# Second attention of a two-layer block: keys made for four heads at a time as even and odd halves, five work banks, the maximum pass spread over half slots

## What is computed

```python
q = (q_in @ Wq + bq).reshape(b, sq, 16, 64).transpose(0, 2, 1, 3)
k = (k_in @ Wk + bk).reshape(b, sk, 16, 64).transpose(0, 2, 1, 3)
v = (v_in @ Wv + bv).reshape(b, sk, 16, 64).transpose(0, 2, 1, 3)
q, k = _rope(q), _rope(k)       # turns dims 2i and 2i+1 by an angle of the position
scores = jnp.einsum('bhqd,bhkd->bhqk', q, k) * (1.0 / np.sqrt(64))
scores = jnp.where(valid[:, None, None, :], scores, -jnp.inf)
attn = jax.nn.softmax(scores, axis=-1)
out = jnp.einsum('bhqk,bhkd->bhqd', attn, v)
return out.transpose(0, 2, 1, 3).reshape(b, sq, 1024) @ Wo + bo
```

## Time and profile before

| | |
|---|---|
| runs, median (lowest to highest) | 2943.0 us (2940.43 to 2944.17) |
| profiled execution, its own time | 2939.36 us |
| its span, first to last instruction | 2937.2 us |
| mean granted clock of TensorE | 0.957 |
| share of the span busy: PE, DVE, ACT, POOL | 90%, 68%, 49%, 47% |

### The profile page before, as it was taken

One profiled execution on the slowest core, in us unless ns is written; L12 is line 12 of the kernel. 1 busy time (PEld: TensorE's weight loads), 2 busy tenths in 40 slices (PEclk: granted clock), 3 DMA queues, 4 the chain that ended last, 5 costly groups with the idle time before them and its releaser, 6 DMA issues. The chain is left out here.

```text
span 2937.2 us, 82056 instructions
## 1 busy us (share of the span) xinstructions
PE 2638.0 (90%) x32600; PEld 1569.0 (53%) x32600; DVE 2006.5 (68%) x6348; ACT 1450.8 (49%) x2243; POOL 1374.3 (47%) x1221
## 2 busy tenths in 40 slices
PE   3679999999989569999999999999999999996598
PEld 2423333333355536666666666666666666664365
DVE  3468888888856567667766766766667667662655
ACT  2247777777744035546446455455464454443222
POOL 2000000000000038877878878878778788785100
PEclk8789999999989779999999999999999999998799
DMA  5421111111010110000000000000000000001000
GB/s 156 144 89 24 24 27 22 25 22 25 21 30 1 64 37 7 19 13 7 18 13 7 17 13 7 26 5 19 13 8 18 13 7 7 7 2 51 0 0 15
DMA packets 109630, 75.20 MB, mean 26 GB/s; under 512 B 43907, under 2 KB 101579, under 8 KB 108752
## 3 DMA queue, kind: packets, MB, share of 16 engines
q1 hardware_dynamic: 109264, 70.08, 8.5%
HBM read 56.61 MB, written 13.43 MB: 24 GB/s over the span
## 5 line engine op out<-in xcount | busy, mean ns | idle before, releaser
L1485 ACT ACTIVATE a_probs<-psS 128x1024 f32<-128x1024 f32 (+1 forms) x448 | 431.7, 964 | 630.0 <-PE psS L1366 625.9
L645 ACT ACTIVATE a_probs<-psS 128x1024 f32<-128x1024 f32 (+2 forms) x512 | 443.5, 866 | 207.0 <-PE psS L586 206.6
L1802 POOL TENSOR_TENSOR a_acc<-a_acc,a_probs 128x512 f32<-128x512 f32 x320 | 407.3, 1273 | 225.1 <-ACT a_probs L1485 221.9
L1389 PE MATMUL psX<-a_probs,a_values 128*64 128x256 f32 x3328 | 445.6, 385 | 1.6
L672 DVE CUSTOM_DVE_ANT_0 a_junk<-psT,a_mask 128x384 f16<-128x384 f32 (+1 forms) x683 | 378.2, 573 | 61.3 <-PE psT L562 41.6
L1804 POOL TENSOR_TENSOR a_acc<-a_acc,a_probs 128x512 f32<-128x512 f32 x320 | 407.1, 1272 | 25.1
L1646 DVE CUSTOM_DVE_ANT_0 a_junk<-psT,a_mask 128x400 f16<-128x400 f32 (+1 forms) x514 | 282.6, 573 | 153.8 <-PE psS L1341 86.3
L1646 DVE CUSTOM_DVE_ANT_0 a_junk<-psS,a_mask 128x400 f16<-128x400 f32 (+1 forms) x510 | 280.7, 573 | 150.9 <-PE psT L1341 88.3
L974 POOL MEMSET r_ones<- 128x128 f16 x1 | 0.2, 205 | 694.4 <-POOLq L719 694.4
L1389 PEld LDWEIGHTS psX<-a_probs,a_values 128*64 128x64 f32 x3328 | 224.1, 137 | 105.2 <-issue 24.6
L1776 POOL TENSOR_TENSOR a_klo<-a_kt,a_khi 128x400 f16<-128x400 f32 (+1 forms) x256 | 242.7, 948 | 18.6 <-ACT a_khi L1537 18.6
(11 more groups left out here) (332 smaller groups left out, 5561.4 us busy)
## 6 DMA issues: line engine op xcount, KB each, us to landing
a_kd<-p_kst SPq DMA_DIRECT2D x24, 416.0 KB, 3.4
a_wq<-in_wq SPq DMA_DIRECT2D x64, 128.0 KB, 2.1
a_keys<-a_kd SPq DMA_DIRECT2D x96, 75.0 KB
p_ctx<-in_ctx SPq DMA_DIRECT2D x8, 768.0 KB
a_ctx<-in_ctx SPq DMA_DIRECT2D x8, 768.0 KB
a_queries<-a_lowest SPq DMA_DIRECT2D x256, 0.5 KB, 2.0
p_mask_raw<-in_mask_t SPq DMA_DIRECT2D x16, 224.0 KB, 4.4
a_queries<-a_qd SPq DMA_DIRECT2D x64, 52.0 KB
```

The source lines that it names most:

```text
L645: nc.scalar.activation(dst, src, ACT.Exp).then_inc(exp_done, 1)
L1389: ins = nc.tensor.matmul(w.sums[n % 2][64 * hd:64 * hd + 64, 0:T], w.values[:, n % 2, c, 64 * hd:64 * hd + 64], w.probs[:, k % RING1, 2 * ...
L1485: nc.scalar.activation(dst, src, ACT.Exp).then_inc(exp_done, 1)
L1802: nc.gpsimd.tensor_tensor(acc, acc, src[:, :, 0, :], ALU.add).then_inc(sum_step, 1)
```

## The change

1. **Quads.** Keys and queries are made for four heads (a quad, two pairs, `QUADS1` = 32) at a time. The columns of `Wk` and `Wq` are put in the order: all even dimensions of four heads, then all odd ones, so one bank holds 4 x 32 even dimensions and the other the odd ones. The exchanged matrix `wk1x` goes. The rotation works between the two banks: four products and two sums per quarter. In even iterations quarters 0 and 1 of a quad are made, in odd ones quarters 2 and 3, at (slot, half) (0, 0) and (3, 1); the queries in even iterations at (6, 1).
2. **Moved by DMA.** ScalarE and GpSimd put the high part and the remainder into `made_keys` and `made_queries`; SP moves each head's even and odd 32 rows from there to its place in `keys` and `queries`, in four transfers for each group of quarters (32 partitions, high and low parts of up to 801 keys each). TensorE, and ScalarE before it overwrites `made_keys`, wait for these transfers (`keys_in`).
3. **Five banks.** The separate banks of the weighed sums become one (`psO`); the bank so freed joins the ring (`NEAR1` = 5). `spread` becomes a piece of the ring. ScalarE copies the weighed sums away (`take_out`) before the next pair's first weighing; `take_inverse` goes.
4. **Half slots.** TensorE's and VectorE's loops run over (slot, half). Scores stand in half 0, weighing in half 1. The eight units of the maximum pass stand alone at (1,1), (2,0), (2,1), (3,0), (4,1), (5,0), (5,1), (6,0); the values in four blocks. `turn_max` stands at (2, 1). ScalarE's loop still runs over slots.

The diff, cut to its core:

```diff
-AHEAD1 = [2, 2, 1, 1, 1, 1, 0]
-VALUES1 = {2: (0, 1), 4: (2, 3)}
-ITERATIONS1 = range(-3, PAIRS1 + 1)
+HALVES1 = [(sl, half) for sl in range(SLOTS1) for half in range(2)]
+UNITS1 = {(1, 1): 0, (2, 0): 1, (2, 1): 2, (3, 0): 3, (4, 1): 4, (5, 0): 5, (5, 1): 6, (6, 0): 7}
+VALUES1 = {(1, 0): 0, (3, 0): 1, (4, 0): 2, (6, 1): 3}
+KEY_TIMES1 = {(0, 0): 0, (3, 1): 1}
+NEAR1 = 5
+ITERATIONS1 = range(-4, PAIRS1 + 1)
...
+            def give_keys(n, js):
+                sp.wait_ge(k_lo, 4 * (n // 2) + js[-1] + 1)
+                made, at0 = made_at(js[0])
+                o, width = QUARTER_AT[js[0]], sum(QUARTER[j] for j in js)
+                for src, dst, part in blocks(n):
+                    sp.dma_start(w.keys[dst, n % KEPT1, :, o:o + width],
+                                 made[src, :, part, at0:at0 + width]).then_inc(keys_in[n % KEPT1][part_of(n, js[0])], 16)
...
+                    if sl == 0 and is_pair(it + 3):
+                        if it >= 1:
+                            sp.wait_ge(b_full, SLOTS1 * it)
+                        give_queries(it + 3)
+                        give_keys(it + 3, (0, 1))
+                        if it % 2 == 0:
+                            give_keys(it + 3, (2, 3))
+                    if it % 2 == 1 and sl in (2, 5) and is_pair(it + 3):
+                        give_keys(it + 3, (2 if sl == 2 else 3,))
...
+                c0 = (2 * (q % 4) + part) * P
                 for i, (split, moving) in enumerate(((0, hi), (1, hi), (0, lo))):
-                    for hd in range(2):
-                        c0 = p * P + 64 * hd
-                        ins = nc.tensor.matmul(out[64 * hd:64 * hd + 64, 0:width], w.wk[:, part, split, c0:c0 + 64], moving,
-                                               start=(i == 0), stop=(i == 2), skip_group_check=True)
+                    ins = nc.tensor.matmul(out[:, 0:width], w.wk[:, split, c0:c0 + P], moving, start=(i == 0), stop=(i == 2))
...
             for it in ITERATIONS1:
-                for sl in range(SLOTS1):
-                    if is_pair(it):
+                for sl, half in HALVES1:
+                    if half == 0 and is_pair(it):
                         scores(it, sl)
...
+                    if half == 1 and sl > 0 and is_pair(it):
+                        weigh(it, sl - 1)
+                    if is_pair(it + 2) and (sl, half) in UNITS1:
+                        for hd in range(2):
+                            ahead(it + 2, UNITS1[sl, half], hd)
...
-                    if is_pair(it + 1) and sl == 1:
+                    if is_pair(it + 1) and (sl, half) == (2, 1):
                         turn_max(it + 1)
...
+            def key_hi(q, j):
+                for part in range(2):
+                    act.wait_ge(near_free[bank_of(("key", q, j, part))], uses_of(("key", q, j, part)))
+                if q > 0:
+                    wait_given(act, 2 * q - 2, j)
+                    wait_given(act, 2 * q - 1, j)
...
                     if is_pair(it):
                         exponent(it, sl)
+                    if is_pair(it - 1) and sl == 0:
+                        take_out(it - 1)
...
                     if is_pair(it + 1) and sl == 1:
                         take_max(it + 1)
-                    if is_pair(it - 1) and sl == 4:
-                        take_inverse(it - 1)
...
+                nc.vector.scalar_tensor_tensor(w.swung[:, 0, 0:width], even, bias[:, 0:1], w.sin[:, cols], ALU.add, ALU.mult)
+                nc.vector.scalar_tensor_tensor(even, even, bias[:, 0:1], w.cos[:, cols], ALU.add, ALU.mult)
+                nc.vector.scalar_tensor_tensor(w.swung[:, 1, 0:width], odd, bias[:, 1:2], w.sin[:, cols],
+                                               ALU.add, ALU.mult).then_inc(k_step, 1)
+                dve.wait_ge(k_step, 2 * done + 1)
+                nc.vector.tensor_tensor(w.kt[:, j % 2, 0, 0:width], even, w.swung[:, 1, 0:width],
+                                        ALU.subtract).then_inc(near_free[bank_of(names[0])], 1)
+                nc.vector.scalar_tensor_tensor(odd, odd, bias[:, 1:2], w.cos[:, cols], ALU.add, ALU.mult).then_inc(k_step, 1)
+                dve.wait_ge(k_step, 2 * done + 2)
+                nc.vector.tensor_tensor(w.kt[:, j % 2, 1, 0:width], odd, w.swung[:, 0, 0:width],
+                                        ALU.add).then_inc(near_free[bank_of(names[1])], 1)
```

More of the change, by code:

```diff
@@ L1097, in leaves_in, with quad_in, quarter_in, split_in @@
     return it // PER_BATCH - 1 if it % PER_BATCH == 0 and it >= PER_BATCH else None
+def quad_in(it):
+    m = (it + 4) // 2
+    return m if it >= -4 and m < QUADS1 else None
+def quarter_in(it, sl, half):
+    return it % 2 * 2 + KEY_TIMES1[sl, half] if (sl, half) in KEY_TIMES1 and quad_in(it) is not None else None
+def split_in(it, sl):
+    return it % 2 * 2 + (0 if sl == 2 else 1) if sl in (2, 5) and quad_in(it) is not None else None
+def query_in(it):
+    return quad_in(it) if it % 2 == 0 else None
+def query_split_in(it):
+    return quad_in(it) if it % 2 == 1 else None
 def count_pieces():
@@ L1103, in count_pieces @@
     for it in ITERATIONS1:
-        for sl in range(SLOTS1):
-            if is_pair(it + 2):
-                order += [("ahead", it + 2, u, hd) for u in units_ahead(sl) for hd in range(2)]
-            if turned_in(it) is not None and 2 <= sl <= 5:
+        for sl, half in HALVES1:
+            if is_pair(it + 2) and (sl, half) in UNITS1:
+                order += [("ahead", it + 2, UNITS1[sl, half], hd) for hd in range(2)]
+            if turned_in(it) is not None and 2 <= sl <= 5 and half == 1:
                 order.append(("turn", turned_in(it), sl - 2))
[L1109 to L1114, removed]
-            if is_pair(it + 1) and sl == 1:
+            if is_pair(it + 1) and (sl, half) in VALUES1:
+                order.append(("value", it + 1, VALUES1[sl, half]))
+            if query_in(it) is not None and (sl, half) == (6, 1):
+                order.append(("query", query_in(it)))
+            if quarter_in(it, sl, half) is not None:
+                order += [("key", quad_in(it), quarter_in(it, sl, half), part) for part in range(2)]
+            if is_pair(it + 1) and (sl, half) == (2, 1):
                 order.append(("max", it + 1))
-            if is_pair(it - 1) and sl == 3:
+            if is_pair(it - 1) and (sl, half) == (3, 0):
                 order.append(("sums", it - 1))
-            if leaves_in(it) is not None and sl >= 5:
+            if is_pair(it - 1) and (sl, half) == (4, 1):
+                order.append(("spread", it - 1))
+            if leaves_in(it) is not None and sl >= 5 and half == 1:
                 order.append(("project" if sl == 5 else "leave", leaves_in(it)))
@@ L1250, in _ @@
             load_masks(1)
-            for n in range(2):
-                load_queries(n)
+            for q in range(2):
+                load_queries(q)
             for it in ITERATIONS1:
@@ L1407, in spread @@
             def spread(n):
+                out = piece(("spread", n))
                 pe.wait_ge(rec_done, n + 1)
@@ L1760, in weights_lo @@
             def weights_lo():
-                pool.wait_ge(w_hi, 3)
-                for i in range(3):
+                pool.wait_ge(w_hi, 2)
+                for i in range(2):
                     hi, lo = weights(i)
```

408 lines of the change are left out of this document (205 added, 203 removed).

## The result

The changed kernel takes **3007.5 us** (median, 3004.9 to 3009.0) beside 2943.6 for the kernel before on the same chip: ratio 1.0217, 95% interval 1.0199 to 1.0235. It is slower by 64 us; the forecast was 80 faster, with a range that ended at 2930.

A forecast was written before the change was run, and what follows sets the result against it. TensorE was taken to set the 23.72 us iteration. Plain iterations -89, projection -11, tail -2, prologue +6 and DMA +16 sum to -80: 2863 us from the median 2943.0, own range 2832 to 2895, overall range 2805 to 2930.

The forecast's parts named there:

- the DMA term: ScalarE's key copy in slot 2 of even iterations waits for SP's transfers: +16 us in all (0 to 35).
- the context's load ahead of them: In seven even iterations the context's load precedes the key transfers, making the copy 0.4 to 3 late: 12 us.
- rival 3: Transfers set the time at ScalarE's slot 2 key copy in even iterations, deciding from an issue of 0.64: 3002 us, chance 0.06.
- the plain period: Plain iterations of the second attention, one pair of heads each, fall by 1.49 from 23.72 to 22.2: -89 us over 60.
- The sentence on the ports: Transfers within 32 partitions reach 8 of 16 ports, some 218 GB/s; by it the transfers' sum would be +15 at most.
- The wait of the moved transpose: TensorE waits before slot 3's scores for an exponential queued behind ScalarE's copy of the maxima: 1.4 us added per plain iteration.
- The keys: TensorE's key blocks of 0.51 us go from eight per pair to eight per quad: 2.04 us saved per plain iteration.
- a rotation: On VectorE, a quad's rotation of four products and two sums takes 3.64 us, against 1.95 for a pair's before.
- rival 2: VectorE holds the key banks longer and delays TensorE's maximum units: 67 us back, 2930 us (2890 to 2945), chance 0.12.
- The projection: Seven iterations carrying a batch's output projection lose TensorE's wait: 7 x (2.04 - 0.43), -11 us.
- 0.1 on each: Some three added changes of kind of product on TensorE, 0.1 us each: 0.3 added per plain iteration.
- The prologue: From the first key product to the first exponential, added rotations on VectorE cost +6 us (0 to 12).

The follow-up runs named there:

- e4_both: Changed kernel with ScalarE's copy of the maxima behind slot 2's exponential and an odd pair's first transfers issued earlier, on three semaphores: 2830.8 us, 0.9628 of the kernel before.
- e7_context_only: Changed kernel with only the next context loaded, normalised and turned one iteration earlier: 3017.0 us, 1.0252 of the kernel before.

## Why the prediction was wrong

**The step that failed** is the DMA term, "so TensorE feels only a copy that starts after 12.0 ... I put 0.15 x 30 = 4.5", in all +16. Its place and its chain were right: last quarter's remainder, then 4 + 1 + 12 issues, then landing. Its terms against iteration 22: start 2.13 after the scores (forecast 1.9), 12.28 for 17 issues (7.3), last landing to copy 1.75 (2.0): 16.16 in place of 11.2. ScalarE wanted the copy at 9.71 (9.6). So one number was off, the duration of an issue: 0.43 had been taken between two rows of other transfers, and it is 0.597, with the gap 0.64, and with one long issue (1.95) in this chain a mean of 0.72. In the loop the transfers cost 80.5 in place of 16: 43.1 in iterations 0 of eight, where the forecast had 12 for the context's load ahead of them, and 36.8 in iterations 6, against 4.5 for all 30. In 2 and 4 they cost 0.7 together, as other waits cover them, which the forecast had not seen either. The break-even that the text gave was 0.64. It had this very number as the point from which rival 3 decides, and gave it 0.06, on nothing but the many small transfers at 0.343 and 0.476; neither row is of the kind that the change issues, so the chance was too low for what was known. That rival 3's 3002 came within 6 us is in part luck: it had 144 from 30 iterations by an issue of 0.761, where the loop has 80.5 from half of them, and 37 for the context and 32 for the plain period (below) make up the rest. The sentence on the ports (Trainium skill, SBUF — State Buffer, "Door 1: The DMA port swizzle") did not decide: 50 KB more lengthened the median landing from 1.98 to 2.21, an estimated 225 GB/s beside the page's 218, which agrees, but bytes were not what the queue waited for.

**What the sum left out.** First the clock: in iteration 22 the loss against the version without the wait is 28.46 - 23.19 = 5.27, of which 3.63 is idle; the other 1.64 is work at the lower clock behind it (TensorE is busy for 23.43 in place of 21.80). Second a wait that no part of the prediction names: a quad's keys begin one and a half iterations sooner than a pair's did, and the new batch's context is not ready. Bare, it costs 4.4 in each of seven iterations (26.17 to 21.73); in the changed kernel it and the wait for the transfers cover each other, so that taking away either alone disappointed.

**What was right.** The wait of the moved transpose: 1.4 forecast, 1.40 in the row, 1.46 in the odd period, 89 to 95 us in two pairs of runs. The keys: blocks of 0.52, half as many. VectorE: a rotation 3.57 beside 3.64, and its waits at the units gone with five banks; rival 2 is out, and the run with four banks shows what it would have been. GpSimd's remainder 1.71 beside 1.7. The projection: iteration 0 takes 27.17 - 23.19 = 3.98 more than a plain even one where the waits are off, beside 29.40 - 23.73 = 5.67 before: 1.69 gained, 1.61 forecast.

**What was off by a size.** With both waits off a plain iteration takes 22.74 in the mean (22.28 and 23.19), 0.54 above 22.2. Most of it is the term "0.1 on each" change of kind, 0.3 in all: by the starts of its blocks, an odd iteration of `e4_both` has 6.64 of weighing beside 6.26 before, 2.62 of values beside 2.39 and 6.02 of scores beside 5.84, together 0.79 more in place of 0.3. A weighing behind a key block had been short, 0.86 from start to start; behind a value block it takes 1.01 (before, then `e4_both`). This is read from the traces; no run tested it.

```profile
1433.77 1.03 PE L1389 MATMUL psX<-a_probs,a_values 128*64 128x256 f32 x8
1434.63 0.58 PE L1402 MATMUL psT<-ones,a_acc 128*64 128x1 f32 x16
```

```profile
1425.31 1.08 PE L1473 MATMUL psX<-a_probs,a_values 128*64 128x256 f32 x8
1426.32 0.34 PE L1427 MATMUL psT<-a_keys,a_queries 64*128 64x400 f16 x1
```

**The account** of the loop, first exponential to that of pair 63: 1563.8 before, 1621.9 after, where the sum has about 1478. Of the 144 between, the transfers are 1621.9 - 1541.4 = 80.5 (in their place the forecast had 16), the context another 1541.4 - 1504.2 = 37.2, the plain period 0.54 x 60 = 32, and some 10 remain that I have not placed. These are differences of one traced execution each; by the medians of the runs the transfers are 78 and the context 45. The prologue came 10 later to its first exponential, where 6 was forecast; over the variants it varies by 9 (1102.3 to 1111.1), and its cause stays open.

## What to carry to other kernels

Where a copy on an in-order engine overwrites a buffer that transfers must leave, count the issues ahead of the last transfer, price them one by one, and look at what is queued behind the copy: here moving the copy two slots took the whole wait away, and in iteration 6 so did a semaphore that counts only the transfers that matter. When a forecast depends on one unknown duration and its break-even lies between the rows at hand, both sides deserve a real chance. And after a stall is taken away, look at each kind of iteration for itself: here, in two of four kinds of even iteration, a second wait covered the first.

## What the hardware showed that was not expected

The issue of a transfer between parts of the on-chip memory, 32 partitions at either end, took at least 0.585 on SyncE's queue whether it moved 32, 50 or 100 KB, beside medians of 0.343 and 0.476 for other transfers; and the load of 128 KB behind such transfers (L1280) took 0.58 in the median, where in the kernel before its issue had taken 0.33. Why, no run here shows. And an idle of TensorE of 2.95 or 3.63 left it at a mean granted clock of 0.62 and 0.57 over the next 4 us, most of them at the 1.2 GHz level, while the 1.40 in odd iteration 21 left it at 1.00. An idle of 2.68 did either: in `e7_context_only` iterations 25 and 33 have the same waits, and one kept its clock, the other not, for 2.4 us more:

```profile
1761.75:1786.89 25.14, 21.06 (x252) 12.63 (x251) 18.42 (x55) 18.67 (x33) 17.34 (x14) 1.00 0.13 31
1970.56:1998.11 27.55, 23.47 (x252) 13.73 (x251) 18.34 (x55) 18.77 (x32) 17.33 (x14) 0.88 0.12 29
```
